# Attention and mixture-of-experts kernel: eight wrapped key tiles in place of nine, and another order of work per pair of heads

## The reference, cut to what matters

```python
win = jnp.arange(nb)[:, None] * BLOCK - half + jnp.arange(2 * BLOCK)[None, :]   # 128-row blocks, 256 keys each
scores = jnp.where(valid, einsum('nhbqd,nhbkd->nhbqk', qb, kb) / sqrt(d), NEG)
ctx = einsum('nhbqk,nhbkd->nhbqd', softmax(scores), vb)
idx = [0] + top 62 tokens by the norm of q + [t - 1]                             # per head
g_ctx = softmax(q[idx] @ k.T / sqrt(d)) @ v
ctx[idx] = g_ctx
```

## Time and profile before

| | |
|---|---|
| median of 3 runs | 803.9 us (802.71 to 804.18) |
| the profiled execution, its time | 804.47 us |
| its span, first to last instruction | 802.7 us |
| TensorE clock granted, mean | 0.985 of full |
| busy: PE, PE weight loads | 762.6 us (95%), 644.6 us (80%) |
| busy: DVE, ACT, POOL | 565.4 us (70%), 435.9 us (54%), 228.5 us (28%) |
| attention stage | from about 169 to 380 us of the span |

### The profile page before, as it was taken

The page is one execution under the profiler, slowest core; times in us unless marked ns, Lnnn a source line. Parts: engine busy times, 40 slices in busy tenths (PEclk is TensorE's granted clock), DMA queues, the critical chain, the costliest instruction groups (busy, mean ns, idle before and its releaser), DMA issues.

```text
span 802.7 us, 15555 instructions
## 1 busy us (share of the span) xinstructions
PE 762.6 (95%) x5781; PEld 644.6 (80%) x5781; DVE 565.4 (70%) x1200; ACT 435.9 (54%) x906; POOL 228.5 (28%) x291
## 2 busy tenths in 40 slices
PE   6999999979999999998999998999999999999994
PEld 5787787768777777776888886999999999887884
DVE  5764898558998668787587535666677666659576
ACT  5464352437777776787354334666666566632120
POOL 3400010523555657767355322000000000013122
PEclk9999999998999999999899999999999999999998
DMA  7789555974788789862269431777778787546344
GB/s 236 224 271 354 187 175 175 271 220 118 212 219 219 199 236 262 229 173 78 94 207 350 178 122 66 220 227 231 220 205 250 217 256 214 174 137 216 126 158 144
DMA packets 117644, 161.99 MB, mean 202 GB/s; under 512 B 17380, under 2 KB 65508, under 8 KB 117568
## 3 DMA queue, kind: packets, MB, share of 16 engines
q1 hardware_dynamic: 113984, 153.02, 63.0%
q0 software_dynamic: 3584, 7.97, 3.3%
HBM read 106.98 MB, written 54.79 MB: 202 GB/s over the span
## 4 chain that ended last, share of the span: by engine, by line
PE 38%; issue 33%; DVE 9%; DMA 7%; POOL 6%; ACT 4%; SPq 2%; POOLq 0%; DVEq 0%; ACTq 0%
PE bank L1234 27%; PE wide L1234 7%; POOL PA L2204 3%; DMA scr_qtok<-H2A 2%; DMA scr_q<-hl 1%; PE wide L1243 1%; DMA H2A<-scr_oe,FG 1%; PE bank L1407 1%; DMA QSl<-scr_q 1%; DVE MX L1859 1%; DMA QSe<-scr_q 1%; DVE NRM L1813 1%; POOL STC L2136 1%; DVE MX L1862 1%; DMA WQH<-MR 1%
## 5 line engine op out<-in xcount | busy, mean ns | idle before, releaser
L1234 PE MATMUL wide<-W2H,HH 128*128 128x512 f32 x308 | 100.7, 392 | 0.5 <-ACT OUTR L1535 0.5
L2204 POOL TENSOR_TENSOR PA<-PT 128x512 f32<-128x512 f32 x64 | 81.2, 1280 | 62.1 <-ACT PT L1617 61.6
L1702 ACT ACTIVATE SIL<-bank 128x256 f32<-128x256 f32 (+1 forms) x72 | 32.6, 453 | 99.3 <-PE bank L1234 99.0
L2023 DVE TENSOR_TENSOR SIL<-bank,SIL 128x256 f32<-128x256 f32 (+1 forms) x72 | 36.9, 512 | 69.4 <-ACT SIL L1702 69.0
L1234 PE MATMUL bank<-XT,W13H 128*128 128x256 f32 (+1 forms) x336 | 76.6, 322 | 0.0
L1535 ACT ACTIVATE HH<-SIL 128x256 fp32r<-128x256 f32 (+1 forms) x72 | 35.2, 489 | 64.2 <-DVE SIL L2023 64.2
L1234 PEld LDWEIGHTS wide<-W2H,HH 128*128 128x128 f32 x308 | 57.8, 188 | 13.0 <-ACT OUTR L1535 1.3
L2245 POOL DMA_INDIRECT H2A<-scr_oe,FG x8 | 8.0, 996 | 208.9 <-issue 208.9
L1234 PE MATMUL wide<-W2L,HH 128*128 128x512 f32 x168 | 65.8, 391 | 0.3 <-DVE W2L L1934 0.3
L2025 DVE TENSOR_TENSOR HH<-SIL,HH 128x256 fp32r<-128x256 f32 (+1 forms) x72 | 37.0, 514 | 40.0 <-ACT HH L1535 40.0
L2136 POOL TENSOR_TENSOR STC<-STC,mhalf 128x1 f32<-128x1 f32 x47 | 29.8, 633 | 107.4 <-DVE STC L1736 107.3
(11 more groups left out here) (310 smaller groups left out, 2159.9 us busy)
## 6 DMA issues: line engine op xcount, KB each, us to landing
R<-in_L_ffn_W_dram SPq DMA_DIRECT2D x48, 512.0 KB, 5.6
scr_q<-hl SPq DMA_DIRECT2D x16, 512.0 KB, 4.0
scr_k<-hl SPq DMA_DIRECT2D x16, 512.0 KB, 4.0
R<-in_L_ffn_sw_dram SPq DMA_DIRECT2D x12, 512.0 KB, 4.7
QSe<-scr_q SPq DMA_DIRECT2D x36, 128.0 KB, 3.5
KSe<-scr_k SPq DMA_DIRECT2D x36, 128.0 KB, 3.6
R<-_attn_hidden_states_dram SPq DMA_DIRECT2D x16, 256.0 KB, 3.6
scr_qtok<-H2A SPq DMA_DIRECT2D x16, 256.0 KB, 3.9
```

The source lines that it names most:

```text
L1234: return pe.matmul(ps, a, b, start=start, stop=stop, skip_group_check=True)
L1702: sc.activation(sil.buf[r, 0:N], a_in, ACT.Silu).then_inc(*a_inner.up("silu", q, m))
L2023: dv.tensor_tensor(sil[r, 0:N], b_in, sil[r, 0:N], ALU.mult).then_inc(*d_inner.up("mul", q, m))
L2204: po.tensor_tensor(hold["pa", n, a].buf[:, :], hold["pt", n, a].buf[:, :], hold["pt", n, a + 2].buf[:, :], ALU.add).then_inc(*g_add.up(n, a))
```

## The change

The keys of a batch become a circle. `scr_k` gets 64 columns more a batch (`KEYS` = 1088), in front of the sequence, into which its last 64 keys are stored a second time (eight small stores in the projections). A key tile has 1088 columns. Tile t is columns 128t to 128t + 127; tile 0 holds the last 64 and the first 64 keys and serves the first and the last block of queries in one product of 256 columns. The exponential of this joint tile is taken in two pieces of 128 columns with either end's mask. In the value tile the same holds: tile 0's halves are the two ends, and the ninth tile and two blocks of zeros go. `global_turn` has eight transposes in two groups, `global_values` 16 products.

The exponentials of units 2 and 3 go to a wide tile (`PE`, 1024 columns, in order of query); `local_add` now waits for both units. In the diff:

```diff
-        TILES = ([0, 1, 2, 3], [4, 5, 6, 7], [8])
+        TILES = ([0, 1, 2, 3], [4, 5, 6, 7])
         UNITS = (((1, 0, 0, 256), (3, 256, 256, 512)), ((5, 512, 0, 256), (7, 768, 256, 512)),
-                 ((0, 0, 0, 128), (2, 128, 128, 384), (4, 384, 384, 512)),
-                 ((4, 512, 0, 128), (6, 640, 128, 384), (8, 896, 384, 512)))
-        EDGE = {2: (0, P, 512), 3: (384, 0, 384)}
+                 ((2, 128, 0, 256), (4, 384, 256, 512)), ((6, 640, 0, 256),))
+        JOINT_COLS = ((256, 0, 1), (384, SEQ - P, 0))
...
                 for t, q0, c0, c1 in UNITS[u]:
-                    k0 = min(max(0, 128 * t - 64), SEQ - P)
-                    ins = mm(ps.buf[:, c0:c1], kb.buf[0:97, k0:k0 + P], qb.buf[0:97, q0:q0 + c1 - c0], True, True)
+                    ins = mm(ps.buf[:, c0:c1], kb.buf[0:97, t * P:(t + 1) * P], qb.buf[0:97, q0:q0 + c1 - c0], True, True)
+                if u == 3:
+                    ins = mm(ps.buf[:, 256:512].rearrange("p (z q) -> p z q", z=2), kb.buf[0:97, 0:P],
+                             both_ends(qb.buf[0:97, :]), True, True)
...
-                w.wait_ge(*g_const.at("edge"))
-                e0, o0, o1 = EDGE[u]
-                sc.activation(pt.buf[:, e0:e0 + P], ps[:, e0:e0 + P], ACT.Exp, bias=edge[:, u - 2:u - 1], scale=SCALE)
-                sc.activation(pt.buf[:, o0:o1], ps[:, o0:o1], ACT.Exp, scale=SCALE).then_inc(*a_exp.up(n, u))
+                elif u == 2:
+                    sc.activation(pt.buf[:, P:640], ps[:, :], ACT.Exp, scale=SCALE).then_inc(*a_exp.up(n, u))
+                else:
+                    w.wait_ge(*g_const.at("edge"))
+                    sc.activation(pt.buf[:, 640:896], ps[:, 0:256], ACT.Exp, scale=SCALE)
+                    for c0, q0, e in JOINT_COLS:
+                        ins = sc.activation(pt.buf[:, q0:q0 + P], ps[:, c0:c0 + P], ACT.Exp, bias=edge[:, e:e + 1], scale=SCALE)
+                    ins.then_inc(*a_exp.up(n, u))
...
                 w.wait_ge(*a_exp.at(n, a))
-                w.wait_ge(*a_exp.at(n, a + 2))
+                for u in (2, 3):
+                    w.wait_ge(*a_exp.at(n, u))
...
+                if n == 1 and g4 % 2:
+                    sp.dma_start(kd[:, c * P:(c + 1) * P, g4 // 2 * KEYS:g4 // 2 * KEYS + WRAP].rearrange("l p t -> p l t"),
+                                 f(hb.buf[:, :, 512 - WRAP:512])).then_inc(*hl.slots[hb.i].up(g4, n, c, "wrap"))
```

More of the change, by code:

```diff
@@ L552, in local_exp @@
             def local_exp(n, u):
-                hold["pt", n, u] = PT.take()
-                hold["pt", n, u].done(p_val, n, u // 2)
-                hold["pt", n, u].done(g_add, n, u % 2)
+                if u < 2:
+                    hold["pt", n, u] = PT.take()
+                    hold["pt", n, u].done(p_val, n, 0)
+                    hold["pt", n, u].done(g_add, n, u)
+                elif ("pe", n) not in hold:
+                    hold["pe", n] = PTE.take()
+                    hold["pe", n].done(p_val, n, 1)
+                    for a in range(2):
+                        hold["pe", n].done(g_add, n, a)
             def local_add(n, a):
@@ L1010, in pair_on_sp @@
                 slot(5)
-                slot(6)
+                head("local_exp", i, 0, 2)
+                head("local_exp", i, 0, 3)
+                head("local_exp", i, 1, 1)
+                head("local_exp", i, 1, 0)
+                head("row_copy", i + 1, 0)
+                pair("global_exp", i)
+                head("local_exp", i, 1, 2)
+                head("local_out", i, 0)
+                head("local_exp", i, 1, 3)
+                pair("global_turned", i, 0)
+                pair("stack_copy", i + 1)
@@ new lines, in pair_on_pool @@
+            def pair_on_pool(i, slot):
+                slot(0)
+                slot(1)
+                slot(2)
+                pair("scatter_rows", i - 2, 0)
+                head("local_add", i, 0, 1)
+                head("local_add", i, 0, 0)
+                slot(3)
+                pair("scatter_rows", i - 2, 1)
+                pair("stack_split", i + 1)
+                slot(4)
+                slot(5)
+                head("local_add", i, 1, 1)
+                slot(6)
+                head("local_add", i, 1, 0)
+                slot(7)
+                pair("gather", i + 2)
@@ L1012, in pair_on_sp @@
+            def pair_on_sp(i, slot):
+                slot(0)
+                head("store_heads", i - 1, 1)
+                pair("load_values", i + 1)
+                head("row_send", i + 1, 0)
+                head("store_heads", i + 1, 0)
+                slot(1)
+                head("load_queries", i + 2, 1)
+                slot(2)
+                head("load_keys", i + 2, 1)
+                slot(3)
+                slot(4)
                 head("load_keys", i + 3, 0)
+                slot(5)
@@ L1413, in global_values @@
                 w.let_go(ps.free)
-                for r in range(3):
+                for r in range(2):
                     w.wait_ge(*a_glob.at("t", i, r))
```

220 lines of the change are left out of this document (89 added, 131 removed).

## The result

The changed kernel takes **817.45 us** (median of 4 runs, 813.15 to 818.71) beside 804.04 (802.71 to 806.69) of the kernel before: ratio **1.014, 95% interval 1.0113 to 1.0166**. The forecast was 797.6; it is slower instead, and outside the range. The profiled execution took 818.71 us (span 816.9, clock 0.970, where before had 804.47, 802.7 and 0.985). One run of a later experiment (e8: 864.69 us at a mean clock of 0.845) was a slow one and is in none of the figures.

A forecast was written before the change was run, and what follows sets the result against it. VectorE was taken to bound the top-k pairs, TensorE with its waits the later ones. TensorE pairs -1.9, crowded pairs -3.9 and start -0.5 made -6.3 us; from the median of 803.9 that gave 797.6, range 793.5 to 803.8.

The forecast's parts named there:

- L: Landing time of the 4 KB row of shifts: 3.8 us in the TensorE stretch, 4.4 crowded; bounds 2.4 and 5.64.
- 8.2 + 3.8 = 12.0: Forecast period of the four TensorE-bound pairs, loop plus landing, against 12.48 us before: -1.9 us in all.
- 8.2 + 4.4 = 12.6: Forecast period of the five crowded pairs, loop plus landing, against 13.38 us before: -3.9 us in all.
- The loop: Second head's scores, ScalarE's queue, TensorE's work, row copy, issue and landing: a pair takes at least 8.2 us plus L.
- issue 0.1: Loop's term for issuing the row's send after ScalarE's copy: 0.1 us.
- the slower rival: Attention pairs: the loop becomes the bound and costs more than the waits it replaces; 811 us, chance 0.15.
- (L between 3.4 and 4.6) give 794.5 to 801: The forecast's own bounds on the whole time, for landings of the row between 3.4 and 4.6 us.
- Last pair and hand-over ... 0.: End of attention, hand-over to the feed-forward part: POOL's chain sets it and stays, change 0.
- TensorE's own work: TensorE's work in one attention pair falls from 11.5 to 11.2 us with eight key tiles.
- The 0.45 for a late bank: TensorE's wait for a free bank before the stack transpose: 0.45 us on 11.2, own period 11.65.
- Top-k pairs 0: The five pairs bound by VectorE's top-k steps keep their work and nearly their order: change 0.
- By 2 us the loop would be 10.2 and would never bind.: With the Trainium skill's nearly constant 2 us for a small transfer, the pairs' loop would take 10.2 us and not bind.

The follow-up runs named there:

- e8: Kernel before, with the rows of shifts sent by ScalarE on its own queue instead of by SP: 822.78 us, ratio 1.0222.
- e5: Changed kernel, with the first context tile's mean and the load of tile 2 in slot 3 of pair 10 instead of slot 0: 814.79 us, ratio 1.0123.
- e10: Kernel before, with the row of shifts sent once into each query buffer and not for later heads: 807.74 us, ratio 0.9987.
- e14: Changed kernel, row sent once into each query buffer, SP still waiting at the place of every later send: 804.06 us, ratio 0.9967.
- e2: Data of the kernel before (nine key tiles) in the changed kernel's new order: 818.28 us, ratio 1.0142.
- e17: Changed kernel, with only the feed-forward weight loads moved behind the second row's send and the queries on SP: 808.56 us, ratio 1.0018.
- e4: Changed kernel, with the second head's finish of the pair before ahead of slots 2, 3 and 4 on VectorE: 818.51 us, ratio 1.0143.
- e12: Changed kernel, row sent once into each query buffer, first tile's mean late, last head's finish ahead of the chores: 807.89 us, ratio 0.9987.
- e6: Changed kernel, with the rows of shifts sent by ScalarE on its own queue right behind its copy: 835.26 us, ratio 1.0338.
- e9: Changed kernel, with the row of shifts sent once into each query buffer and not for later heads: 807.82 us, ratio 0.998.

## Why the prediction was wrong

The step that failed is "L: ... I take 3.8 for the TensorE stretch ..., 4.4 for the crowded one", and the term made from it, "8.2 + 3.8 = 12.0" and "8.2 + 4.4 = 12.6". It took L from the kernel before, for a change that puts more loads ahead of the send, and put one mean where each pair has its own. The mechanism, a loop closed by the landing, is the one it names.

- *The loop.* Right, and nearly its size: 7.82 us outside the landing where 8.1 was put (8.2 with the issue), shown by e5 and by its fall to 7.2 when the copy moved. It is not new, though: by e8 the old order has it with some 7.6. There it hardly bound: the old order's pairs 6 to 9 took 12.1 to 12.8 us with rows and without them (e10), where the new order's take 11.2 or less in three of four (e14). With it the changed kernel's own pairs come out. Landings of pairs 7 to 10 and 12 are 5.90, 3.73, 5.33, 6.87 and 6.63; with 7.82 they give 13.7, 11.6, 13.2, 14.7 and 14.5. Measured 15.12, 11.56, 13.15, 16.76 and 18.22. Where there was no half clock (8 and 9) it fits to 0.1 us.
- *L as one number.* This is what was wrong, twice over. For pairs 6 to 9 the mean landing was 4.66 us, not 3.8. In the kernel before it was 3.71 in these pairs and in e2, the new order with keys of the old length, 4.55: 3.8 fitted the old order and not the new one. For pairs 10 to 14 it was 3.95, below my 4.4, and the stretch still lost 5.9 us: a pair takes the larger of its own period and 7.8 plus its landing, and a mean of 3.95 made of 6.87, 2.47, 6.63, 1.80 and 1.99 gains nearly nothing in three pairs and loses in two. The landing had to be put into the maximum pair by pair. Part of it is not the transfer's way but "issue 0.1": SP was still issuing loads when the row was ready, 0.74, 0.66 and 2.49 us late in pairs 7, 10 and 12. Which pairs are in danger can be read off SP's queue: the loads ahead of the send, of which e17 moved some. I took the size from one send and from transfers of other tiles; the trace before has every row, and its second rows landed in 1.8 to 5.5 us.
- *The point of decision.* "It decides from L = ... 4.3 us in the TensorE pairs ... about 4.1 in the top-k pairs" was the slower rival, at 0.15, with 811. It is what happened, with landings up to 6.87 instead of the 5.3 at its upper end, so its price too was low. The range left it out: "(L between 3.4 and 4.6) give 794.5 to 801" is not what the terms give. At 3.4 they give 793.7; at 4.6 the top-k pairs bind as well, by the same text, and it is 804.4.
- *What the rival lacked: the clock.* TensorE's granted clock fell from 2.4 to 1.2 GHz at long waits: 17 us of half clock between 266 and 345 us, none there before. Pair 12 is 3.8 us longer than the loop gives, with 9.2 us of half clock in it; in e4 pair 7 is 3.7 longer than 7.82 and its landing of 5.42 give, with 8.7. So a long wait is paid again, with about 0.4 us per microsecond of half clock. No sum of mine had it, though the text listed it as a sign.
- *"Last pair and hand-over ... 0."* Wrong by 2.7 us: 17.5 became 20.2, in all the kernels with circle and new order but without an early finish 19.6 to 20.7. Those with it took 18.2 to 19.5 (e4 18.5), so about half of it is the last head's finish behind the chores on VectorE. With nine tiles (e2) it was 18.2 without an early finish; what the circle adds there was not followed up.
- *The crowded pairs' other wait.* The context tile on VectorE was in no term: 4.78 us idle, 4.0 of it TensorE's. e5 took it away, and the row bound pair 10 in its place (16.25 us for 16.76). The 2.7 us between the medians of different batches are not told from nothing by the ratios' intervals (1.0140 and 1.0123).
- *TensorE's own work.* 11.2 was right: 11.14 in e14. The 0.45 for a late bank on top of it was not there. Eight tiles, two-instruction units and POOL's slack did what was said; nothing was wrong on that side.
- *Top-k pairs 0.* Nearly: +0.6 for five, with pair 3 at 12.95 behind a landing of 4.91. *Start -0.5.* The first stack came 1.0 earlier and the first pair was 1.8 shorter; in other kernels of this order 0.6 to 1.7.
- *Waits for queries gone, waits for POOL gone.* Right.
- *"By 2 us the loop would be 10.2 and would never bind."* The section of the Trainium skill cited there speaks of transfers that GpSimd issues; the rows are SP's. The shortest landings, 1.74 to 1.8 us, are near its figure, the mean of the second rows in pairs 6 to 9 more than twice it.

Open: how much of the longer landing the three key loads make that the new order put ahead of the send (no run puts them back alone), why e12's pairs 7 and 9 stall without a named wait, and whether the 5.4 us in the feed-forward part is scatter alone.

## What to carry to other kernels

Where an order makes a small transfer part of a loop, write the period as the larger of two times for each turn, with that turn's own landing, and judge the landing by what the new queue holds ahead of it, not by a median of other transfers or by the old queue. The cure that worked here was neither an earlier copy nor a second queue but the place of the bulk loads: behind the send, not ahead of it; and what they are moved ahead of next pays in its turn. Price a long wait with the clock that it may cost as well: behind the 2.3 us of pair 7 there were 3.41 us at half clock, and the pair was 1.4 us longer than its loop.

## What the runs showed of the hardware that was not expected

- From issue to landing a 4 KB row sent from SP took 1.74 us at best and 7.75 at worst (both in e2); moving loads from ahead of it to behind it shortened it (e17). The Trainium skill, page "DMA: Bandwidth & Descriptors", section "Queues, rings and completion order", says that an engine consumes the descriptors of a ring in their order: e17 agrees, where the row passed the weight loads and nothing else was changed. The Trainium skill's section "Latency and other measured facts", on the same page, has 0.2 us on average and 2 us at high load for an access to HBM. The row goes from SBUF to SBUF, only the loads ahead of it read HBM, so no run here tests that figure; the 6 us between the best and the worst are more than it.
- A second issuing queue made it worse: 4.3 us from issue to landing on average in e6 for 2.9 in the changed kernel, and 8.55 at worst for 6.21. The Trainium skill, the same page, section "Issuing engines are not separate DMA queues", says that it would save only the issuing engine's time. The runs say more: here it lengthened the landing, and by 0.86 us the loop through the engine that issued.
- When SP no longer waited for rows at all (e9, e12), its loads ran ahead and the DMA engines' share went from 0.85 to 1.00 in the crowded stretch. Held at its old places (e14) it was 0.87, and the four TensorE pairs took 46.0 us instead of e9's 50.7. In the whole time the two differ by 0.1% only, by their ratios, which the intervals don't tell apart. So it is a sign, not shown, that an issuing engine's waits can do good by pacing the loads.
